# Block 0's start in a macaron kernel: the mus' transposes moved between the two halves of the first transposed tiles, and their two loads between the x tiles

## The reference, cut to what matters

```python
def _L0_ffn_ref(x, W_r, W_k, W_v, mu_r, mu_k):
    x_prev = jnp.concatenate([jnp.zeros((B, 1, C), x.dtype), x[:, :-1, :]], axis=1)
    xr = mu_r * x + (1.0 - mu_r) * x_prev
    xk = mu_k * x + (1.0 - mu_k) * x_prev
    r = jax.nn.sigmoid(jnp.einsum('btc,dc->btd', xr, W_r))
    k = jnp.einsum('btc,dc->btd', xk, W_k)
    k_act = jnp.square(jax.nn.relu(k))
    return r * jnp.einsum('btc,dc->btd', k_act, W_v)
...
x = x + 0.5 * _L0_ffn_ref(_layernorm(x), ...)
x = x + _L0_attn_ref(_layernorm(x), ...)
x = x + 0.5 * _L0_ffn_ref(_layernorm(x), ...)
```

## Time and profile before

| what | value |
|---|---|
| median of 3 runs | 313.1 us (312.91 to 313.57) |
| the profiled execution's own time | 313.04 us |
| its span, first to last instruction | 311.3 us |
| PE busy | 303.8 us, 98% of the span |
| DVE, ACT, POOL busy | 240.4, 235.3, 214.1 us |
| mean granted TensorE clock | 0.997 |

### The profile page before, as it was taken

How to read it: one execution, slowest core, us unless ns; L and a number is a source line. 1 busy time by engine, 2 the same in 40 slices (tenths; PEclk the granted TensorE clock), 3 DMA queues, 4 the chain that set the end, 5 groups by cost and what they waited for, 6 DMA issues and landing times.

```text
span 311.3 us, 5822 instructions
## 1 busy us (share of the span) xinstructions
PE 303.8 (98%) x2044; PEld 276.2 (89%) x2044; DVE 240.4 (77%) x586; ACT 235.3 (76%) x461; POOL 214.1 (69%) x236
## 2 busy tenths in 40 slices
PE   6999999999999999999999999999999999999995
PEld 5688889989988988988989998989999999999884
DVE  3989894675756846995894699586979797999695
ACT  2896959779589579679359448669797979699981
POOL 4487977779678687669169314815798979758833
PEclk9999999999999999999999999999999999999998
DMA  7970000000000000000000000000002010101134
GB/s 215 356 241 0 1 3 0 0 2 0 3 0 3 0 0 2 0 2 0 0 3 1 2 0 0 2 1 3 0 3 67 2 67 20 50 2 66 33 106 135
DMA packets 10752, 10.85 MB, mean 35 GB/s; under 512 B 482, under 2 KB 10724, under 8 KB 10724
## 3 DMA queue, kind: packets, MB, share of 16 engines
q1 hardware_dynamic: 10432, 10.23, 10.1%
q10 hardware_dynamic: 292, 0.26, 0.3%
HBM read 6.29 MB, written 4.19 MB: 34 GB/s over the span
## 4 chain that ended last, share of the span: by engine, by line
PE 89%; DVE 6%; ACT 2%; issue 1%; POOL 0%; DVEq 0%; POOLq 0%; ACTq 0%
PE psK L1270 8%; PE psK L1271 8%; PE psK L1272 8%; PE psX L1270 8%; PE psRV L1272 8%; PE psRV L1270 8%; PE psRV L1271 8%; PE psX L1271 7%; PE psX L1272 7%; PE psA L1287 4%; PE psX L1487 2%; PE psK L1474 2%; PE psA L1474 2%; PE psX L1401 2%; PE psRV L1512 1%; PE psRV L1377 1%
## 5 line engine op out<-in xcount | busy, mean ns | idle before, releaser
L939 DVE SCALAR_TENSOR_TENSOR mix<-psA,mu,mix 128x512 f32<-128x512 f32 x60 | 41.5, 744 | 11.6 <-ACT mix L626 11.6
L609 ACT ACTIVATE xn<-xs,shiftA,rstdA 128x256 f32<-128x256 f32 x53 | 27.7, 607 | 15.8 <-POOL shiftA L402 15.8
L418 POOL TENSOR_TENSOR mix_k_lo<-mix,mix_k_hi 128x512 fp32r<-128x512 f32 x26 | 33.3, 1298 | 8.7 <-ACT mix_k_hi L659 8.7
L626 ACT ACTIVATE mix<-psA,one_mu 128x511 f32<-128x511 f32 x60 | 36.9, 698 | 0.6 <-PE psA L1287 0.6
L1270 PE MATMUL psRV<-ffn_hi,mix_r_hi 128*128 128x256 f32 x120 | 34.2, 285 | 0.0
L1272 PE MATMUL psRV<-ffn_hi,mix_r_lo 128*128 128x256 f32 x120 | 33.5, 279 | 0.0
L1271 PE MATMUL psRV<-ffn_lo,mix_r_hi 128*128 128x256 f32 x120 | 33.4, 279 | 0.0
L1270 PE MATMUL psRV<-ffn_hi,act_hi 128*128 128x256 f32 x96 | 27.4, 286 | 0.0
L1272 PE MATMUL psRV<-ffn_hi,act_lo 128*128 128x256 f32 x96 | 26.8, 279 | 0.0
L1271 PE MATMUL psRV<-ffn_lo,act_hi 128*128 128x256 f32 x96 | 26.8, 279 | 0.0
L470 POOL TENSOR_TENSOR k_lo<-k_tok,k_hi 128x512 fp32r<-128x512 f32 x14 | 18.1, 1294 | 11.6 <-ACT k_hi L713 11.6
(11 more groups left out here) (204 smaller groups left out, 1084.0 us busy)
## 6 DMA issues: line engine op xcount, KB each, us to landing
xs<-x_dram SPq DMA_DIRECT2D x7, 512.0 KB, 8.6
out_dram<-xs SPq DMA_DIRECT2D x7, 512.0 KB, 3.0
out_dram<-xs SPq DMA_DIRECT2D x4, 128.0 KB, 1.8
xs<-x_dram ACTq DMA_DIRECT2D x2, 128.0 KB, 3.0
xs<-x_dram SPq DMA_DIRECT2D x2, 128.0 KB, 2.8
silu_u<-w_ffn_k_dram SPq DMA_DIRECT2D x1, 256.0 KB, 4.6
silu_u<-w_ffn_r_dram SPq DMA_DIRECT2D x1, 256.0 KB, 6.3
q_store<-w_k_dram SPq DMA_DIRECT2D x1, 256.0 KB, 6.5
```

The source lines that it names most:

```text
L418: nc.gpsimd.tensor_tensor(mix_k_lo[:, h, :], mix[:, 0, h, :], mix_k_hi[:, h, :].bitcast(F32), ALU.subtract).then_inc(s_lo_k, 1)
L609: nc.scalar.activation(xn[:, t, :], tile_row(xs, b, t), ACT.Identity, bias=shiftA[:, t:t + 1], scale=rstdA[:, t:t + 1]).then_inc(s_xn, 1)
L626: nc.scalar.activation(mix[:, rk, h, 1:BLOCK], psA[:, h, 0:BLOCK - 1], ACT.Copy, scale=one_mu[:, rk, h:h + 1]).then_inc(s_prev, 1)
L939: nc.vector.scalar_tensor_tensor(out=m, in0=psA[:, h, :], scalar=mu[:, rk, h:h + 1], in1=m, op0=ALU.mult, op1=ALU.add).then_inc(s_mix, 1)
```

## The change

The load of mu_k moves from ACT's queue to SP's, between tiles 0 and 2, and that of mu_r stays on ACT's queue but goes between tiles 1 and 3. The 20 + 2 transposes that nobody reads become 26 in one piece ahead of everything. The mus' transposes stand behind the first half's transposes (g = 0) instead of ahead of both halves. On DVE the normalized tiles 0 and 1 are made ahead of one_mu and mu, tiles 2 and 3 behind them. What is computed stays the same.

```diff
@@ block.sync
-            for t in (0, 2):
-                sp.dma_start(tile_row(xs, 0, t), x[t * P:(t + 1) * P, :]).then_inc(s_x0[t], 16)
+            sp.dma_start(tile_row(xs, 0, 0), x[0:P, :]).then_inc(s_x0[0], 16)
+            sp.dma_start(mu_rows[0:1, :], mu_k.rearrange("p h -> (p h)").unsqueeze(0)).then_inc(s_mu_in, 16)
+            sp.dma_start(tile_row(xs, 0, 2), x[2 * P:3 * P, :]).then_inc(s_x0[2], 16)
@@ block.scalar
-            for t in (1, 3):
-                act.dma_start(tile_row(xs, 0, t), x[t * P:(t + 1) * P, :]).then_inc(s_x0[t], 16)
-
-            for rk, given in enumerate((mu_k, mu_r)):
-                act.dma_start(mu_rows[rk:rk + 1, :], given.rearrange("p h -> (p h)").unsqueeze(0)).then_inc(s_mu_in, 16)
+            act.dma_start(tile_row(xs, 0, 1), x[P:2 * P, :]).then_inc(s_x0[1], 16)
+            act.dma_start(mu_rows[1:2, :], mu_r.rearrange("p h -> (p h)").unsqueeze(0)).then_inc(s_mu_in, 16)
+            act.dma_start(tile_row(xs, 0, 3), x[3 * P:4 * P, :]).then_inc(s_x0[3], 16)
@@ block.vector
-            def normalize_some(n):
+            def normalize_some(n, tiles=range(TILES)):
...
-                for t in xn_vector[n]:
+                for t in tiles:
+                    if t not in xn_vector[n]:
+                        continue
...
+            normalize_some(0, (0, 1))
             dve.wait_ge(s_mu_t, 1)
...
-            normalize_some(0)
+            normalize_some(0, (2, 3))
@@ block.tensor
-            keep_clock_up(20)
-            pe.wait_ge(s_mu_in, 32)
-            for h in range(HALVES):
-                last = nc.tensor.transpose(psK[:, 0, 2 * h:2 * h + 2],
-                                           mu_rows[:].rearrange("r (p h) -> r h p", h=HALVES)[:, h, :], ident[0:2, 0:2])
-            last.then_inc(s_mu_t, 1)
-            keep_clock_up(2)
+            keep_clock_up(26)
             for g in range(2):
...
                     last.then_inc((s_t0, s_tA)[g], 1)
+                if g == 0:
+                    pe.wait_ge(s_mu_in, 32)
+                    for h in range(HALVES):
+                        last = nc.tensor.transpose(psK[:, 0, 2 * h:2 * h + 2],
+                                                   mu_rows[:].rearrange("r (p h) -> r h p", h=HALVES)[:, h, :],
+                                                   ident[0:2, 0:2])
+                    last.then_inc(s_mu_t, 1)
```

## The result

The changed kernel takes 314.12 us (median of 10 runs, 313.26 to 314.54), the kernel before 313.52 us in as many (312.91 to 313.74); the ratio is 1.0022, 95% interval 1.0012 to 1.0032 (here and below ratios compare the means, the times given are medians). It is slower by 0.6 us by the medians and 0.7 by the means, about twice the +0.31 that I had worked out, just outside my range (312.7 to 314.1) and on the side of "slower", which I had given 0.19.

A forecast was written before the change was run, and what follows sets the result against it. DVE's mixes, then PE, were taken to bound the kernel; the third mix's delay of 0.31 us, added to the profiled 313.04, gave 313.35, and with 0.06 up to the median 313.4 us. Range 312.7 to 314.1.

The forecast's parts named there:

- What bounds: DVE's mixes from 8.92, dense PE from 14.25: one us of DVE's mixes is one us of the kernel.
- PE's spare transposes: Start of PE's work: 22 become 26, the six further ones cost 6 x 0.11 us, the 26th starts at 6.99.
- The prediction's own sign of being wrong: Wrong if the 17th spare transpose is not where the spacing halves; two further signs concerned xn and the third mix.
- Rival B: All 26 spare transposes stay at the lower level, 0.21 us apart: about +1.4, 314.5 us; chance 0.05.
- the sentence beside it: Beside rival B: the clock's rise varies by half a us between runs, moving the sum by 0.25 either way.
- The mus' pair and one_mu: Behind the first half's transposes: the pair starts at 7.63, one_mu at 8.06, 1.10 us later than before.
- From one_mu to the third mix: The sequence takes 1.96 us, so the third mix starts at 10.02 instead of 9.71: +0.31 us.
- DVE idle ahead of the third mix: After the second mix DVE idles from 9.66 to 10.02, waiting for tile 3.
- The loads: Tiles 2 and 3 issued up to 0.54 us later, xn 1 done by 6.7, still ahead of PE; costed at nothing.
- D: Tiles 2 and 3, or a mu, come late: +0.5, 313.6, or 314.1 with a full us; chance 0.10.
- A, the order pays: one_mu before 7.75 makes the third mix earlier: -0.1 to -0.3, 312.8 to 313.0 us; chance 0.14.
- C, the clock falls in the gap of 0.64: PE's gap behind the mus' pair, about 0.6 us, slows the next 16 matmuls: about +3.0, 316.4; chance 0.04.

The follow-up runs named there:

- after_again: The changed kernel profiled once more, no edit: 313.08 us.
- loads_only: The kernel before with only the new order of the loads, a mu between the two x tiles of each queue: 313.42 us, ratio 1.0000.
- old14: The kernel before with 14 instead of 20 spare transposes ahead of the mus: 312.20 us, ratio 0.9972.
- old8_split_mus: old8 with the mus' loads shared between the queues, behind both x tiles of each: 312.46 us, ratio 0.9973 against the kernel before.
- old14_again: The same kernel as old14, run again: 312.23 us, ratio 0.9970 against the kernel before.
- old14_tail5: old14 with 5 instead of 2 spare transposes behind the mus' pair: 312.28 us, ratio 0.9970 against the kernel before.
- old8: The kernel before with 8 instead of 20 spare transposes ahead of the mus: 312.04 us, ratio 0.9959.

## Why the prediction was wrong

- **What bounds** held: the third mix's shift reached block 1's transposes (15.44 - 14.25 = 1.19 for 1.18), and with them the time (1.06).
- **PE's spare transposes, the step that failed.** "The six further ones cost 6 x 0.11: the 26th starts at 6.99" took the spacing of one execution whose clock rose early for a property of the kernel. With 20 or more spare ones the profiles show rises from 5.5 to 8.5 us. Where all are slow, 20 end 0.5 us later than in the early case (4.53 against 4.00 us) and 26 a whole us later (5.69 against 4.63 us). So the six cost 4.63 - 4.00 = 0.63 us in the one case and 5.69 - 4.53 = 1.16 us in the other, and the third mix moves by +0.13 or +0.64. The cost that I had taken for certain was the low end of a spread; the sum should have been a mean over the moments of the rise. The prediction's own sign of being wrong came true: the spacing halved at the last spare transpose and not at the 17th.
- **Rival B** had this outcome (all 26 at 0.21) with a chance of 0.05. Its premise was that transposes never bring the clock up, and in before, after_again and loads_only the spacing halved while PE ran nothing else. The cause, a rise that falls on different moments from execution to execution, was in the sentence beside it, with 0.25 us either way. The half us of spread behind that figure is too small here: the same changed kernel rose at 5.9 and at 8.0, and its third mix moved by 1.05 us. "The kernel before is hit less" was right, and the difference of the medians, 0.60, fits the +0.64 of two late executions. How often each kernel rises late was not counted by profiles.
- **The mus' pair and one_mu** held: the pair 0.20 behind the fourth transpose, one_mu 0.43 behind the pair (8.66, 9.09); with an early rise 8.03 for 8.06.
- **From one_mu to the third mix** I had 1.96 us; it took 1.80 (9.09 to 10.89) and 1.81 (8.03 to 9.84). A small error in the change's favour.
- **DVE idle ahead of the third mix**: mixes that follow each other start 0.40 us apart, so with the first at 9.88 the third could have started at 10.68; it started at 10.89. The idle time that I forecast is there, 0.21 us instead of 0.36.
- **The loads** cost nothing: right, but with less cover than I had worked out. Tile 3's statistics started at 5.76 and 5.68 in the two profiles against 4.71 before, about a whole us later where I had allowed 0.54, and xn 1 was done at 7.02 and 6.94 instead of 6.7. With the early rise PE wanted it from 7.07 on, so the cover was down to about 0.1 us. D didn't come.
- **A, the order pays**: the mechanism is real, my count hid it. With 20 ahead in both, all at the lower level, the new order has the third mix 0.50 earlier: one_mu comes 0.44 later (7.94 against 7.50), and the chain from it to the third mix is 1.81 instead of 2.75. With 14 ahead, where xn bounds, the new order is the later one.
- **C, the clock falls in the gap of 0.64**: in no profile.

## What to carry to other kernels

Spare work that is meant to bring an engine's clock up is on the critical path as soon as the real operands are ready before it ends; here twelve of the twenty transposes could go, and the kernel with 8 is faster than the kernel before (0.9959), which is faster than the changed one. A spacing read from one execution of a kernel that starts at the lower clock is one draw: look at a second profile before a sum is made of it. A change of order and a change of a count in one edit can hide each other; here -0.5 and +1.1 us at the third mix, in the executions with a late rise.

## What was not expected of the hardware

The moment of the rise. In the eight profiles with 20 or more spare transposes from 2.60 on it came near 5.5, 5.9 (twice), 7.0, 7.6, 8.0, 8.1 and 8.5 us. In the six with 14 or 8 it came near 5.7 and 6.5 in two, and inside ffn_k(0), at 9.7 to 11.3 us, in four (4.34 to 4.88 us for it instead of 3.69). So the spare ones may well buy an earlier rise; six profiles don't prove it, and no kernel without any was run. But with 8 or 14 the kernel is faster all the same, since the late rise cost only 0.45 us with 14 (312.75 against 312.30). Block 1's transposes started 0.85 us later there, but the xn were ready before PE came to them and they took 1.04 us instead of 1.64, so ffn_r(0) started only 0.24 us later (15.32 against 15.08).

Two executions fell far out and are in no ratio: one of old14 with 610.07 us, whose mean granted clock nevertheless reads 1.00, and one of the kernel before, beside old8_split_mus, with 505.46 us at a mean granted clock of 0.56. Neither has a trace, so what happened in them isn't shown. As such an execution came with 20 spare ones too, and not again in the 30 executions of old14_again, old14_tail5, old8 and old8_split_mus, it isn't shown to have to do with their number; whether fewer make it likelier stays open.
